# Mask products of the routed experts: four feature tiles on four 32-row groups of TensorE, in place of four products of 72 rows

## The reference, cut to what matters

```python
def expert(muW, gW, gqa, gqb, gs, uW, uqa, uqb, us, dW, dqa, dqb, ds, w):
    xe = x + w @ muW.T          # w: tokens x 8 scores, muW: 512 x 8
    gate = jax.nn.silu(_fused_linear(xe, gW, gqa, gqb, gs, w))
    up = _fused_linear(xe, uW, uqa, uqb, us, w)
    return _fused_linear(gate * up, dW, dqa, dqb, ds, w)
outs = jax.vmap(expert, ...)(mask_up_W, gate_W, ..., soft)
```

## Time and profile before

| | |
|---|---|
| median of 3 runs | 1880.67 us |
| the profiled execution | 1881.12 us |
| its span, first to last instruction | 1879.1 us |
| granted TensorE clock, mean over the span | 0.967 |
| TensorE busy / VectorE busy | 1763.9 / 1234.4 us |
| mask products | 128 of 14528 products |
| expert stage | about 600 to 1879 us |

### The profile page before, as it was taken

One profiled execution on the slowest core, in us unless ns is written; L12 is line 12 of the kernel. 1 busy time (PEld: TensorE's weight loads), 2 busy tenths in 40 slices (PEclk: granted clock), 3 DMA queues, 4 the chain that ended last, 5 costly groups with the idle time before them and its releaser, 6 DMA issues.

```text
span 1879.1 us, 36975 instructions
## 1 busy us (share of the span) xinstructions
PE 1763.9 (94%) x14528; PEld 1447.0 (77%) x14528; DVE 1234.4 (66%) x1943; ACT 709.4 (38%) x1492; POOL 265.0 (14%) x237
## 2 busy tenths in 40 slices
PE   4889987899995999999999999999999999999997
PEld 4778865788884787778888888888888888888886
DVE  4677864677765556676675675766766766756776
ACT  4555642122212434343343443533433533434331
POOL 1344544333331000000000000000000000000000
PEclk9888987899997999999999999999999999999999
DMA  4021221000002003030030030020210300300011
GB/s 154 27 63 49 65 68 51 25 12 22 11 0 75 23 9 84 14 93 25 7 94 8 8 94 7 33 68 13 64 35 8 87 13 7 94 7 13 8 51 45
DMA packets 51088, 76.74 MB, mean 41 GB/s; under 512 B 9152, under 2 KB 27712, under 8 KB 50240
## 3 DMA queue, kind: packets, MB, share of 16 engines
q1 hardware_dynamic: 51008, 75.62, 13.3%
HBM read 68.78 MB, written 6.82 MB: 40 GB/s over the span
## 4 chain that ended last, share of the span: by engine, by line
PE 63%; DVE 2%; issue 2%; ACT 1%; POOLq 0%; POOL 0%; DVEq 0%
PE pair L1870 9%; PE pair L1871 9%; PE pair L1872 9%; PE y_ps L1870 3%; PE y_ps L1872 3%; PE y_ps L1871 3%; PE qa_ps L1870 3%; PE qa_ps L1872 3%; PE qa_ps L1871 3%; PE pair L2007 2%; PE pair L1998 2%; PE pair L1997 2%; PE pair L2006 1%; PE qd_ps L2074 1%; PE qd_ps L2075 1%
## 5 line engine op out<-in xcount | busy, mean ns | idle before, releaser
L1870 PE MATMUL pair<-XH,GUH 128*128 128x512 f32 x800 | 313.5, 392 | 0.0
L1871 PE MATMUL pair<-XL,GUH 128*128 128x512 f32 x800 | 312.7, 391 | 0.0
L1872 PE MATMUL pair<-XH,GUL 128*128 128x512 f32 x800 | 312.6, 391 | 0.0
L1870 PEld LDWEIGHTS pair<-XH,GUH 128*128 128x128 f32 x800 | 150.7, 188 | 32.2
L1872 PEld LDWEIGHTS pair<-XH,GUL 128*128 128x128 f32 x800 | 150.5, 188 | 32.0
L1871 PEld LDWEIGHTS pair<-XL,GUH 128*128 128x128 f32 x800 | 150.6, 188 | 31.6
L1434 POOL TENSOR_TENSOR qb_raw<-qb_raw,qb_scale 128x704 f32<-128x704 f32 x8 | 13.6, 1702 | 1056.6 <-DVE G L1588 923.8
L1784 DVE TENSOR_TENSOR h<-pair,sg 128x512 f32<-128x512 f32 x80 | 55.1, 689 | 132.0 <-ACT sg L1533 130.2
L1444 ACT ACTIVATE HH<-h 128x512 fp32r<-128x512 f32 (+1 forms) x120 | 75.8, 632 | 170.4 <-DVE h L1789 94.1
L1588 DVE TENSOR_TENSOR HL<-h,HH 128x512 fp32r<-128x512 f32 (+1 forms) x120 | 82.9, 691 | 83.7 <-ACT HH L1444 83.7
L1533 ACT ACTIVATE sg<-pair 128x512 f32<-128x512 f32 x80 | 47.8, 598 | 221.2 <-PE pair L1998 197.7
(11 more groups left out here) (337 smaller groups left out, 4192.3 us busy)
## 6 DMA issues: line engine op xcount, KB each, us to landing
gu_raw<-in_gu SPq DMA_DIRECT2D x20, 512.0 KB, 3.8
wrep<-soft_f SPq DMA_DIRECT2D x64, 128.0 KB
dw_raw<-in_dw SPq DMA_DIRECT2D x10, 512.0 KB, 4.4
xT_raw<-in_xT SPq DMA_DIRECT2D x8, 512.0 KB, 4.1
x_raw<-in_x SPq DMA_DIRECT2D x8, 512.0 KB, 4.1
VR<-v_rows SPq DMA_DIRECT2D x32, 128.0 KB, 2.5
out<-xtok SPq DMA_DIRECT2D x4, 1024.0 KB, 4.3
gu_raw<-in_gu SPq DMA_DIRECT2D x10, 384.0 KB, 3.3
```

The source lines that it names most:

```text
L1870: mm(out, wh, xh, start=first, stop=False)
L1871: mm(out, wh, xl, start=False, stop=False)
L1872: return mm(out, wl, xh, start=False, stop=last)
```

## The change

Every feature tile k gets its own group of 32 rows, 32 k to 32 k + 31. In a group, rows 0 to 7 hold high mu (by high scores), rows 8 to 15 high mu (by low scores), rows 16 to 23 low mu (by high scores), and the last 8 zeros. `MUS` becomes [128, 128]: the group is the feature tile and the columns its 128 features. The scores `ws` are needed in all four groups, so they are loaded four times. The product k uses rows 32 k to 32 k + 31 of both operands. DMAs: 12 in place of 3 for `mu_raw` (each 8 x 128) and for `ws` (each 8 x 512). [...]

```diff
-        MUS = sb("MUS", [72, D], F32R)
+        MUS, mu_low = sb("MUS", [P, P], F32R), sb("mu_low", [P, P])
+        lows, signs = sb("lows", [P, 1]), sb("signs", [P, 1])
...
-        mu_raw, qa_raw = sb("mu_raw", [72, D]), sb("qa_raw", [P, KC, P])
+        mu_raw, qa_raw = sb("mu_raw", [P, P]), sb("qa_raw", [P, KC, P])
...
-        ws = sb("ws", [72, 2, TB], F32R)
+        ws = sb("ws", [P, 2, TB], F32R)
...
-                after(sp, w_mu, f)
+                after(sp, w_mu, 2 * f)
                 sp.wait_ge(pool_consts, 2)
-                for r in (0, 32, 64):
-                    sp.dma_start(mu_raw[r:r + K8, :], A["mu"][f, :, :]).then_inc(l_mu, 16)
+                for k in range(KC):
+                    for r in (0, K8, 2 * K8):
+                        sp.dma_start(mu_raw[32 * k + r:32 * k + r + K8, :],
+                                     A["mu"][f, :, k * P:(k + 1) * P]).then_inc(l_mu, 16)
...
-                for r, part in ((0, 0), (32, 1), (64, 0)):
-                    sp.dma_start(ws[r:r + K8, b, :].bitcast(F32),
-                                 soft_hl[part, f, :, tb * TB:(tb + 1) * TB]).then_inc(l_ws[b], 16)
+                for k in range(KC):
+                    for r, part in ((0, 0), (K8, 1), (2 * K8, 0)):
+                        sp.dma_start(ws[32 * k + r:32 * k + r + K8, b, :].bitcast(F32),
+                                     soft_hl[part, f, :, tb * TB:(tb + 1) * TB]).then_inc(l_ws[b], 16)
...
+            nc.gpsimd.memset(lows[:], 1.0).then_inc(pool_consts, 1)
+            pool.wait_ge(pool_consts, 6)
+
+            for u in range(2):
+                for r in range(0, P, 32):
+                    nc.gpsimd.affine_select(out=lows[r:r + 32, :], in_=lows[r:r + 32, :], compare_op=ALU.is_ge, fill=0.0,
+                                            base=(-2 * K8, 3 * K8 - 1)[u], pattern=[[0, 1]],
+                                            channel_multiplier=(1, -1)[u]).then_inc(pool_consts, 1)
+                pool.wait_ge(pool_consts, 10 + 4 * u)
+            nc.gpsimd.tensor_scalar(signs[:], lows[:], -2.0, 1.0, ALU.mult, ALU.add).then_inc(pool_consts, 1)
+            pool.wait_ge(pool_consts, 15)
...
-                        sub(MUS[64:72, :], mu_raw[64:72, :], MUS[64:72, :].bitcast(F32)).then_inc(w_mu, 1)
+                        if not routed:
+                            dve.wait_ge(pool_consts, 15)
+                        nc.vector.tensor_scalar(mu_low[:], mu_raw[:], lows[:, 0:1], None, ALU.mult).then_inc(w_mu, 1)
+                        dve.wait_ge(w_mu, 2 * f + 3)
+                        nc.vector.scalar_tensor_tensor(MUS[:], MUS[:].bitcast(F32), signs[:, 0:1], mu_low[:],
+                                                       ALU.mult, ALU.add).then_inc(w_mu, 1)
...
-                    pe.wait_ge(w_mu, f + 1)
-                    pe.wait_ge(l_ws[tb % 2], 48 * (2 * f + tb // 2 + 1))
-                mm(xe_ps(k, at, routed)[:], MUS[:, k * P:(k + 1) * P], ws[:, tb % 2, :],
+                    pe.wait_ge(w_mu, 2 * f + 2)
+                    pe.wait_ge(l_ws[tb % 2], 192 * (2 * f + tb // 2 + 1))
+                rows = slice(32 * k, 32 * k + 32)
+                mm(xe_ps(k, at, routed)[:], MUS[rows, :], ws[rows, tb % 2, :],
                    start=True, stop=True).then_inc(xe_done, 1)
```

More of the change, by code:

```diff
@@ L1423, in _ @@
             nc.gpsimd.iota(row_i[:], pattern=[[0, 1]], base=0, channel_multiplier=1).then_inc(pool_consts, 1)
-            pool.wait_ge(pool_consts, 5)
+            nc.gpsimd.memset(lows[:], 1.0).then_inc(pool_consts, 1)
[8 more added lines that the diff above has]
+            pool.wait_ge(pool_consts, 15)
             def body(e, routed, nxt):
@@ L1514, in body @@
                     if turn and nxt:
-                        act.wait_ge(l_mu, 48 * (f + 2))
+                        act.wait_ge(l_mu, 192 * (f + 2))
                         after(act, xe_done, KC * (n + 1))
```

## The result

| | before | after |
|---|---|---|
| median | 1880.55 us (5 runs, 1878.65 to 1882.56) | 1871.06 us (5 runs, 1869.16 to 1873.85) |
| profiled execution / its span | 1881.12 / 1879.1 us | 1873.85 / 1872.1 us |

The ratio of the times is 0.9949, with a 95% interval of 0.9937 to 0.9962: 9.5 us less, 0.5% faster. The forecast was 1871.2 us, in a range of 1867.0 to 1875.5.

The account below looks back on a forecast made before the run. The prediction took TensorE's product stream in the routed experts as the bound. 32 groups at 0.295 us gave 9.4 us, all else nothing: profiled execution 1881.12 to 1871.7, median 1871.2 us, range 1867 to 1875.5.

Parts of the forecast that it names:

- The bound: Routed experts, 830 to 1820 us: only TensorE's stream sets the time, busy 989.92 of 990.00 us.
- The group: Four mask products on TensorE: 0.23 together plus 0.41 in and out, 0.64 us for 0.93, over 32 groups.
- its signs: Expected TensorE timeline: starts within 0.02 us, 0.32 in, 0.42 behind; full to full 0.74, then 0.33, for 1.16 and 0.24.
- the four losses: Attention stage, going into and out of 32-row products: 0.09, 0.11, 0.11 and 0.11 us, together taken as 0.41.
- The term taken from 256 columns: Attention-stage `scores` products of 256 columns: overlap and the 0.41 us loss were assumed to hold for 512 columns.
- rival (d): Mask products do not run together: 0.93 stays, 0.41 us a group is added, 13.1 us slower, 1893.8; chance 0.06.
- The signals: Each mask product raising `xe_done`: between nothing and 0.10 us a group, 3.2 us in all; taken as nothing.
- Rival (a): Signals of the mask products cost the full bound: 0.20 us less a group, 6.2 us gained, 1874.5; chance 0.09.
- SyncE, VectorE, ScalarE: Extra DMAs, two VectorE instructions at a turn and ScalarE's shorter copy: hidden by waits or idle time, cost nothing.
- The rule of the drain: TensorE changing tiling mode drains the engine; the 0.09 and the last 0.11 us of loss look like it.
- a visit: TensorE going from 128- or 72-row products to 32-row products and back: 0.41 us lost in emptying and loading.
- the one in the block before the first routed one: Mask group with a VectorE wait between its two pairs: counted like the others, missing by at most 0.93 us.

Follow-up runs that it names:

- one signal: Changed kernel with only the last product of a group raising `xe_done` (the group made in pairs keeps two signals): 1869.72 us, ratio 0.9954 to the kernel before.
- all rows: Changed kernel, but each of the four mask products reads all 128 rows of both operands: 1879.53 us against 1879.74 for the kernel before.
- two visits: Changed kernel with the second pair of mask products moved behind the next tile's first three products: 1891.4 us against 1880.37 for the kernel before.
- three DMAs: Changed kernel with scores loaded into the first row group alone, 3 DMAs a block for 12: 1871.54 us, ratio 0.9962 to the kernel before.
- same 32 rows: Changed kernel with all four mask products of a group reading rows 0 to 31: 1891.76 us against 1880.37 for the kernel before.

## Why the prediction was right

**The bound.** It said that in the routed experts only TensorE's stream sets the time. The stretch after has 970.00 busy of 970.00 us, and the block became shorter by 0.29 where the stream was 0.31 ahead close behind the group.

**The group.** Forecast: 0.23 + 0.41 = 0.64 in place of 0.93, taken as 0.295 less. Measured: 0.29 a block (8.6 us over 30 blocks). The gaps came as written: 0.32 in, 0.42 behind the group, 0.34 after the first full product (0.33 forecast).

The mechanism was right, but the last digit was not earned. First, without rounding the prediction's terms give 0.928 - 0.234 - 0.41 = 0.284, or 9.1 us for 32 groups; 0.295 is rounded up. Second, its signs do not add up to its sum: 0.74 and 0.33 in place of 1.16 and 0.24 is 0.33 less, not 0.295, since the 0.42 behind the group leaves out some 0.03 of the four losses that it had read from the attention stage. Third, the lead over the kernel before is not made in one place: it is 0.31 by the second full product behind the group, 0.26 ten products later (837.56 above), and 0.29 over the whole block. The prediction had no such term, and no run shows where it comes from.

**The term taken from 256 columns.** The step from the attention stage's products of 256 columns to 512 was the weakest link, and was what rival (d) hung on. The four start together and 0.42 later the next product starts. With all four on the same rows, where they don't run together, the block is 0.41 longer than before: that is the case of rival (d), 11.4 us slower for 13.1 worked out.

**The signals.** Rival (a) is refuted by the run with one signal: neither its block nor its gap is shorter by 0.10. The nearest row (72-row products with a signal each at the dense rate) was the better guide. The Trainium skill, page "TensorE: Matmul & The Clock Gate", section "The cost: per-tile semaphore tail", gives about 26 ns for each increment, 0.08 us a group as an estimate from it; the block shows nothing of it, and the most that a stretch inside the block shows is 0.04.

**SyncE, VectorE, ScalarE.** Costed at nothing; the run with all rows, which has every one of these edits, takes the time of the kernel before. Of the two loads the sum was right and the parts were not: nine more `ws` DMAs take 3.2 us (3.8 forecast), nine more `mu_raw` 3.8 (3.1). The two VectorE instructions came out at no cost within a range of -0.3 to +0.7.

**The rule of the drain.** The Trainium skill, "TensorEngine Tiling (Array Packing)", section "Key Properties", says that a change of mode drains the engine. The runs agree: a visit costs 0.41 us there and back, of which, by my reading, a part is the uncovered weight loads. The Trainium skill, page "TensorE: Matmul & The Clock Gate", section "Measured speedup vs the span model", has a factor of 3.07 for four such products, which would be 20 us, an estimate from it; 9.5 were measured, since here each group also pays a visit, 32 times 0.41 us or 13 us.

**The sum over the whole kernel.** 9.5 us between the medians, 9.4 forecast. That they agree within 0.1 is luck: the interval of the ratio is 7.1 to 11.8 us. The traces give 31 groups of 0.287 us, and 0.20 for the one in the block before the first routed one (816.93 to 818.12 from the full product before it to the second behind it, for 814.80 to 816.19), which the prediction counted like the others: 9.1 us. The two profiled executions are 7.3 apart; that is less because the kernel after reached the first mask product at 817.3 where the kernel before was there at 815.0. That part of the program is not touched by the row groups: the same kernel after, run again, was there at 814.9 (more below).

What stays open: that each way costs about 0.10 us for emptying and 0.11 for a weight load is my reading of the starts. No run took one of them away. And in all runs of the set the four products also write four different PSUM banks; that different rows are needed is shown, whether different banks are needed too is not.

## What to carry to other kernels

A product on few rows costs as much as one on all rows, and a visit to another kind costs 0.41 us in a dense stream. Packing pays only if it hides more than that: with 512 columns (0.232 us each) at least two products must disappear behind others in each visit, and two barely pay (0.08 us; with one a visit, "two visits", it is a loss of 0.17 a visit). So gather such products into one visit, and search the profile of the same program for a stretch that already has the kind of product and its way in and out: its starts gave the price of a visit, 0.41 us, which is what the block then showed. To measure an effect of 0.3 us a block, take the distance between two starts many blocks apart, not the time of the run.

## What the runs showed that was not expected

The time of the part ahead of the experts differs from run to run by 9 us, while the blocks behind it repeat within 0.02 us from kernel to kernel where the stream is the same: the first mask product started at 809.0 us with the four on the same rows, at 810.9 with three DMAs, 815.0 before, 817.3 after, 814.9 in the same kernel run again, and 818.0 with all rows. The profiled executions follow this. The two earliest were 4.4 and 4.3 us under the median of their kernel (1887.32 for 1891.76, 1867.27 for 1871.54), the two latest 2.8 and 3.8 above (1873.85 for 1871.06, 1883.37 for 1879.53); the other five started their first mask product at 814.0 to 816.3 and lie between 1.6 under and 3.4 above. So most of the scatter of the times is made ahead of the stage that was changed, and a distance of starts inside the stage is free of it.

The cause is not shown. The clock is the obvious candidate: in this part the granted clock is a mean over times at 1.2 and at 2.4 GHz, where in the experts it is 1.00, and TensorE is idle for some 100 of 800 us. But the clock does not put the kernels in order. The stretch 0 to 800 us of "same 32 rows" (809.0), of "three DMAs" (810.9) and of "all rows" (818.0), columns as in the earlier trace rows:

```profile
0.00:800.00 800.00, 697.39 (x9914) 586.27 (x9915) 516.77 (x835) 294.70 (x806) 242.99 (x229) 0.94 0.14 45
```

```profile
0.00:800.00 800.00, 698.52 (x9906) 587.05 (x9907) 514.78 (x833) 294.61 (x805) 243.08 (x229) 0.93 0.14 44
```

```profile
0.00:800.00 800.00, 694.77 (x9872) 583.66 (x9873) 510.54 (x825) 293.01 (x802) 243.53 (x229) 0.93 0.15 45
```

The earliest had 0.94, but the second and the latest both had 0.93 and are 7 us apart.
